# Second attention in pairs of key chunks, with 46 of its 302 score rows in two row tiles of TensorE

## The reference

```python
h = _layernorm(x, gamma, beta)
Q = (h @ Wq).reshape(B, NQ, N_HEADS, HEAD_DIM)          # 16 heads of 64
K = (context @ Wk).reshape(B, NC, N_HEADS, HEAD_DIM)
V = (context @ Wv).reshape(B, NC, N_HEADS, HEAD_DIM)
attn = jnp.einsum('bihd,bjhd->bhij', Q, K)
attn = jax.nn.softmax(attn, axis=-1) * scale             # scale after the softmax
vals = jnp.einsum('bhij,bjhd->bihd', attn, V).reshape(B, NQ, INNER)
return x + vals @ Wo + bo
```

## Time and profile before

| | |
|---|---|
| runs, median (lowest to highest) | 1092.0 us (1091.74 to 1093.75) |
| profiled execution, its own time | 1092.7 us |
| its span, first to last instruction | 1090.9 us |
| mean granted TensorE clock | 0.963 |
| busy: TensorE, its weight loads | 1011.2 us (93%), 738.5 us (68%) |
| busy: VectorE, ScalarE, GpSimd | 742.7 us (68%), 566.7 us (52%), 377.8 us (35%) |
| score passes of the second attention (lines 1281 to 1283) | 384 each |

### The profile page before, as it was taken

One profiled execution on the slowest core, in us unless ns is written; L12 is line 12 of the kernel. 1 busy time (PEld: TensorE's weight loads), 2 busy tenths in 40 slices (PEclk: granted clock), 3 DMA queues, 4 the chain that ended last, 5 costly groups with the idle time before them and its releaser, 6 DMA issues. The chain is left out here.

```text
span 1090.9 us, 31627 instructions
## 1 busy us (share of the span) xinstructions
PE 1011.2 (93%) x12044; PEld 738.5 (68%) x12044; DVE 742.7 (68%) x1406; ACT 566.7 (52%) x1135; POOL 377.8 (35%) x273
## 2 busy tenths in 40 slices
PE   5956999999999999889679999999999999999997
PEld 2642677777777777646327777777777777777786
DVE  4846888778887787311796676767677676767752
ACT  2632777677776776631444444444445444445442
POOL 4612111121111213020106554445555454555542
PEclk8976999999999999979799999999999999999998
DMA  3504444543445432120021211111011111111100
GB/s 117 129 13 132 130 136 143 146 135 121 133 141 149 136 101 87 31 71 0 1 60 41 57 57 58 43 50 41 35 57 55 55 39 53 39 37 57 35 4 4
DMA packets 47022, 79.90 MB, mean 73 GB/s; under 512 B 6979, under 2 KB 33813, under 8 KB 46965
## 3 DMA queue, kind: packets, MB, share of 16 engines
q1 hardware_dynamic: 46964, 79.11, 24.5%
HBM read 50.93 MB, written 21.96 MB: 67 GB/s over the span
## 5 line engine op out<-in xcount | busy, mean ns | idle before, releaser
L1374 ACT ACTIVATE P<-PS 125x448 f32<-125x448 f32 x384 | 207.1, 544 | 265.1 <-PE PS L1283 263.2
L1264 POOL TENSOR_TENSOR Pl<-P 125x896 f16<-125x896 f32 x128 | 229.9, 1801 | 237.0 <-ACT P L1374 237.0
L1010 DVE TENSOR_REDUCE m<-PS 128x1 f32<-128x500 f32 x336 | 220.6, 674 | 114.9 <-PE PS L1001 113.0
L916 DVE TENSOR_REDUCE m_part<-PS 128x1 f32<-128x500 f32 x336 | 210.3, 672 | 60.5 <-PE PS L818 58.9
L1299 PE MATMUL PS<-cNh,P 125*128 125x97 f16 x1344 | 198.0, 208 | 0.1
L1301 PE MATMUL PS<-cNh,Pl 125*128 125x97 f16 x1344 | 197.4, 207 | 0.0
L1300 PE MATMUL PS<-cNl,P 125*128 125x96 f16 x1344 | 196.8, 206 | 0.0
L894 ACT ACTIVATE Pb<-PS 125x448 f32<-125x448 f32 x384 | 186.0, 547 | 19.7 <-PE PS L793 18.7
L1300 PEld LDWEIGHTS PS<-cNl,P 125*128 125x128 bf16 x1344 | 131.9, 98 | 25.4
L818 PE MATMUL PS<-KH,Qmx 128*128 128x500 f16 x336 | 129.4, 387 | 14.2 <-PEq L690 8.2
L1299 PEld LDWEIGHTS PS<-cNh,P 125*128 125x128 bf16 x1344 | 131.1, 98 | 15.7 <-issue 3.2
(11 more groups left out here) (167 smaller groups left out, 1489.0 us busy)
## 6 DMA issues: line engine op xcount, KB each, us to landing
Kst<-k_halves SPq DMA_DIRECT2D x144, 125.0 KB, 2.8
k_halves<-KH SPq DMA_DIRECT2D x16, 750.0 KB, 3.3
cx<-in_ctx SPq DMA_DIRECT2D x16, 562.5 KB
d_cx<-in_ctx SPq DMA_DIRECT2D x16, 562.5 KB
c_halves<-cHi SPq DMA_DIRECT2D x16, 281.2 KB, 2.7
c_halves<-cLo SPq DMA_DIRECT2D x16, 281.2 KB, 3.1
cTh<-c_halves SPq DMA_DIRECT2D x16, 281.2 KB, 3.1
cTl<-c_halves SPq DMA_DIRECT2D x16, 281.2 KB, 4.0
```

The costliest lines, as they stand in the source:

```text
L916: nc.vector.tensor_reduce(m_part[:, t, part:part + 1], PS[:, 6 + k % 2, 0:SP], AX.X, ALU.max).then_inc(s_reduced, 1)
L1010: nc.vector.tensor_reduce(m21[:, t, part:part + 1], PS[:, S1[k % 2], 0:SP], AX.X, ALU.max).then_inc(n_red, 1)
L1264: nc.gpsimd.tensor_tensor(Pl[:, c % NP], P1[:, c % NP], high, ALU.subtract).then_inc(n_low_p, 1)
L1374: nc.scalar.activation(P1[:, c % NP, half * HALF:(half + 1) * HALF], PS[0:KC, u % 3, 0:HALF], ACT.Exp).then_inc(n_exp, 1)
```

## The change

- Scores: the 96 high-by-high, 96 high-by-remainder and 96 remainder-by-high rows and the 14 rows of the maximum are packed anew. Two passes have 128 rows (kA by qA, kB by qB). The last 32 rows of the remainder keys with the high queries, and the 14 rows of the maximum, are a third pass of 46 rows. It stands in partitions 0 to 45 for the first half of the columns and in 64 to 109 for the second; kC holds the keys twice. Tiles of 64 rows by 128 columns are chosen by these partitions.
- Loads: with this packing a batch has 12 loads instead of 4; the two that the maximum pieces read are issued first, ten smaller ones follow.
- Order: chunks go in pairs (six groups). A group is eight full passes, then the 46-row passes of both chunks, then the values of the pair before. Score halves use four PSUM banks, 0 to 3. The maximum pieces use banks 7 and 6, at places written in a table. After the sixth group only the turned maximum and the values of the last pair are left.
- Batch's ends: the next batch's first three score halves no longer wait for the laid maximum. Both transposes of the batch before come in group 0 with a bank each (6 and 7), both copies follow on ScalarE after that group's exponentials, the remainders and the projection come in group 1.
- Maximum: the top of each query is written to PSUM and both f16 parts are made from there, by three VectorE instructions; the constant LIFT moves into the exponential's bias. The turn is one f16 matmul with 128 output rows.
- Pl: VectorE takes chunk 3 alone, GpSimd the other eleven. The memory for the larger buffers comes from weight buffers of the middle stage that share space.

```diff
+        kA = sb_in(late, "kA", [128, 2, SK], F16)
+        kB = sb_in(late, "kB", [128, 2, SK], F16)
+        kC = sb_in(late, "kC", [96 + MR, 2, SK], F16)
-        O1, W1, S1 = 4, 6, (3, 7)
+        O1, W1 = 4, (6, 7)
+        S0, S1 = (3, 7), (7, 6)
...
+            if half == 0:
+                keys(kA, 0, 0, 0, DC)
+            else:
+                keys(kA, 96, 0, 0, 32)
+                keys(kB, 0, 0, 32, 64)
+                keys(kB, 64, 1, 0, 64)
+                keys(kC, 0, 1, 64, 32)
+                keys(kC, 64, 1, 64, 32)
...
+        PLACES = [(0, 0, 0, 0, 0, 0), (0, 0, 0, 0, 2, 0), (1, 0, 1, 1, 1, 1), (1, 0, 1, 1, 1, 1), (1, 0, 1, 1, 1, 1), (1, 1, 1, 1, 0, 0), (0,) * 6]
-        low_on_dve = [c % 3 == 2 for c in range(NC)]
+        low_on_dve = [c == 3 for c in range(NC)]
...
+                def score(i, par, u):
+                    if u == 0:
+                        pe.wait_ge(n_in[1][par], i * LOADS[1] + LOADS[1])
+                    if u == 2 * GC - 1:
+                        pe.wait_ge(n_mlaid, n + 1)
-                    wait_for(pe, n_exp, n * 2 * NC + u - 2)
+                    wait_for(pe, n_exp, n * 2 * NC + u - 3)
-                    o = PS[0:KC, u % 3, 0:HALF]
-                    pe.matmul(o, cTh[:, par, at], Qh[:, par, cols], start=True, stop=False)
-                    pe.matmul(o, cTh[0:DC, par, at], Ql[:, par, cols], start=False, stop=False)
-                    pe.matmul(o, cTl[:, par, at], Qh[0:DC, par, cols], start=False, stop=True).then_inc(n_st, 1)
+                    o = PS[0:KC, u % 4, 0:HALF]
+                    pe.matmul(o, kA[:, par, at], qA[:, par, cols], start=True, stop=False)
+                    pe.matmul(o, kB[:, par, at], qB[:, par, cols], start=False, stop=True)
+                def score_rests(par, g):
+                    for c in range(GC * g, GC * g + GC):
+                        at = slice(c * KC, (c + 1) * KC)
+                        for half in range(2):
+                            rows_of, cols = slice(64 * half, 64 * half + 32 + MR), slice(64 * half, 64 * half + HALF)
+                            mm = pe.matmul(PS[0:KC, (2 * c + half) % 4, 0:HALF], kC[rows_of, par, at], qC[rows_of, par, cols],
+                                           start=False, stop=True, skip_group_check=True)
+                        mm.then_inc(n_st, 2)
...
+                    def pieces(g, place):
+                        these = BESIDE1[g][place]
+                        if par == 0 and g == 1 and place >= 4:
+                            these = (place - 4,)
+                        for k in these if has_b and has_1 else ():
+                            if has_old and k == 0:
+                                pe.wait_ge(n_ot, b * 2)
+                            if has_old and k == 1 and par == 0:
+                                pe.wait_ge(n_y, i)
+                            score_piece1(pe, i, par, k, S1)
+                    for g in range(NG + 1):
+                        if has_1 and g == NG:
+                            turn_maximum(i, par)
+                        if has_b and g < NG:
+                            for j in range(2 * GC):
+                                score(i, par, 2 * GC * g + j)
+                                if j < 3:
+                                    pieces(g, j)
+                            score_rests(par, g)
+                        if has_b and has_old and g == 0:
+                            turn_output(b - 1, 0)
+                            turn_output(b - 1, 1)
+                        pieces(g, 3)
+                        for j in range(GC):
+                            if has_b and g > 0:
+                                values(i, par, GC * (g - 1) + j, tuple(range(QT)))
+                            if has_b and has_old and par == 0 and g == 1 and j == 0:
+                                project(i - 1)
+                            pieces(g, 4 + j)
...
+                        for u in range(2 * GC * g, 2 * GC * (g + 1)) if has_b else ():
+                            act.wait_ge(n_st, b * 2 * NC + 2 * c + 2)
+                            nc.scalar.activation(P1[:, c % NP, half * HALF:(half + 1) * HALF], PS[0:KC, u % 4, 0:HALF], ACT.Exp, bias=lift[0:KC, 0:1]).then_inc(n_exp, 1)
...
+                        if has_b and has_old and g == 0:
+                            keep_old(i, par, 0)
+                            keep_old(i, par, 1)
...
+                        top1 = PS[:, W1[1], 0:QT]
+                        nc.vector.tensor_reduce(top1, m21[:], AX.X, ALU.max).then_inc(n_mlink, 1)
+                        nc.vector.tensor_scalar(mn1[:, :, 32:32 + QT], spread(top1, 1, 2), -1.0, None, ALU.mult).then_inc(n_mlink, 1)
+                        nc.vector.scalar_tensor_tensor(out=mn1[:, :, 32 + QT:32 + MR], in0=spread(top1, 1, 2), scalar=-1.0, in1=mn1[:, :, 32:32 + QT],
+                                                       op0=ALU.mult, op1=ALU.subtract).then_inc(n_mready, 1)
```

More of the change, by code:

```diff
@@ L22 @@
+import itertools
 from contextlib import ExitStack
@@ L976, in program, with keys, queries @@
         n_st, n_fill, n_red, n_mlink = sem("n_st"), sem("n_fill"), sem("n_red"), sem("n_mlink")
-        O1, W1, S1 = 4, 6, (3, 7)
+        O1, W1 = 4, (6, 7)
+        S0, S1 = (3, 7), (7, 6)
         PIECES1 = [(t, part) for part in range(NSP) for t in range(QT)]
+        LOADS = (32, 160)
         def load_halves(sp, i, par, half, queries_made=None, ahead=False):
             slot, n = (par + 1) % 2, i * 2 + par + 1
[L986 to L990, removed]
+            at, loaded = bass.ds(n, 1), n_in[half][slot]
+            def keys(to, first, part, source, count):
+                sp.dma_start(to[first:first + count, slot:slot + 1, :],
+                             c_halves[at, part, source:source + count].rearrange("b p k -> p b k")).then_inc(loaded, 16)
+            def queries(to, first, part, source, count, at_col=0, heads=slice(0, H)):
+                cols = slice(at_col, at_col + (heads.stop - heads.start) * SQ)
+                sp.dma_start(to[first:first + count, slot, cols].rearrange("p (h q) -> p h q", q=SQ).unsqueeze(1),
+                             QK[source:source + count, part, at, heads]).then_inc(loaded, 16)
+            if half == 0:
+                if not ahead:
+                    wait_for(sp, n_st, (n - 1) * 2 * NC)
+                keys(kA, 0, 0, 0, DC)
[5 more added lines that the diff above has]
+                keys(kC, 64, 1, 64, 32)
@@ L996, in score_piece1 @@
+        def score_piece1(pe, i, par, k, banks):
             slot, n = (par + 1) % 2, i * 2 + par + 1
@@ L1221, in turned_parts @@
             cut, rest = divmod(4 * 128, SQ)
-            src = PS[0:DC, W1]
+            src = PS[0:DC, W1[k]]
             if k == 0:
@@ L1264, in body @@
                             nc.gpsimd.tensor_tensor(Pl[:, c % NP], P1[:, c % NP], high, ALU.subtract).then_inc(n_low_p, 1)
-                        if inside(i, par, 1) and c == 4:
+                        if inside(i, par, 1) and c == 3:
                             slot, n = (par + 1) % 2, b + 1
@@ L1326, in turn_maximum @@
                     pe.wait_ge(n_mready, n + 1)
[L1327 to L1331, removed]
+                    pe.matmul(PS[:, W1[0], 0:128], mn1[:].rearrange("p a c -> p (a c)"), ident16[:], start=True, stop=True).then_inc(n_mturned, 1)
                 def body(i, par):
@@ new lines, in lay_maximum @@
+                        for first, t in ((32, 0), (96, QT - 4)):
+                            m = nc.vector.tensor_tensor(qC[first:first + MR, slot].rearrange("p (t q) -> p t q", t=4),
+                                                        spread(PS[first:first + MR, W1[0], 0:128], 1, 4),
+                                                        spread(tab[first:first + MR, C_MM + t:C_MM + t + 4], 2, 128), ALU.mult)
+                        m.then_inc(n_mlaid, 1)
+                    for g in range(NG + 1):
+                        pieces = list(itertools.chain(*BESIDE1[g])) if has_b and has_1 else []
+                        if has_b and has_old and g == 1:
+                            split_old(i, par, 0)
+                            split_old(i, par, 1)
+                        if has_b and has_old and par == 0 and g == 1:
@@ L1471, in body @@
+                        for k in pieces[2:]:
+                            reduce_piece1(dve, i, par, k, S1)
+                        if has_1 and g == NG:
                             lay_maximum()
```

161 lines of the change are left out of this document (66 added, 95 removed).

## The result

The changed kernel takes 1109.78 us, median of four runs (1108.73 to 1111.32), beside 1092.88 us for the one before, measured beside it: ratio 1.015, 95% interval 1.0135 to 1.0165. It is slower, by 17 us, and lies above the stated range (1079 to 1104). Its profiled execution took 1109.35 us with a span of 1107.6, 16.7 us longer than before.

What follows compares the result with a forecast made beforehand. The prediction took TensorE's queue of passes in the second attention as the bound. Seven pairs +1.2, last batch +0.9, start -1.2 and end -1.7 us gave -0.8, so 1091 us (range 1079 to 1104).

Steps and rivals of the forecast that it cites:

- the walk: Second attention's chain summed through tail, head and middle: odd batches 30.65 us, even 33.33, a pair 0.17 longer than before.
- Saved pass, tile changes: TensorE scores: 5 passes a chunk instead of 6 saves 2.28 us a batch; 12 tile changes cost about 0.095 each.
- Rival 1: Tile changes on TensorE cost little, 0.03 instead of 0.1 us: 10 us less, 1081; chance 0.27.
- The bias operand ... keep counts and sizes: Second attention's exponential with its new bias operand, and the middle stage's moved weights: costed at nothing.
- R1: Start of the 46-row passes in a batch's second group; forecast 3.04 us after those of the first group.
- R0: Start of the 46-row passes in a batch's first group, 1.63 us after the batch's start; the number counts groups.
- The port conflict ... nothing waits for: The conflict avoided by splitting the maximum from PSUM stretches a VectorE step nothing waits for today: costed at nothing.
- The tail: Batch's end, from the last group's 46-row passes: 5.88 us, with TensorE waiting twice for GpSimd, 0.7 us each.
- Once-only terms: Outside the repeating batches: start -1.2 us, last batch +0.9, end -1.7.
- Rival 4: Waits and tile changes cost 0.15 rather than 0.10 us: 9 us more, 1100; chance 0.19.
- Rival 2: TensorE's clock falls after idling at batch ends: 1104 to 1117 us, about 1111; chance 0.09.
- Rival 3: The 46-row passes run one after the other, not side by side: 30 us more, 1121; chance 0.05.

Runs made afterwards that it cites:

- e4: Changed kernel with both 46-row passes of a chunk in the lower row tile, one behind the other: 1135.11 us, ratio 1.0383 to the kernel before.
- e1: Changed kernel with the second attention's exponential called without its bias operand, LIFT left out: 1094.88 us, ratio 1.0021 to the kernel before.
- e2: Changed kernel with GpSimd's subtraction for the next context after chunk 5 instead of chunk 3: 1097.85 us, ratio 1.0043 to the kernel before.
- e3: Changed kernel with the low part of chunk 11 on VectorE, behind the maximum: 1098.2 us, ratio 1.0049 to the kernel before.
- e5: Changed kernel with the next batch's first two score halves moved into the tail's first hole: 1098.14 us, ratio 1.0055 to the kernel before.

## Why the prediction was wrong

Direction, size and range were wrong: "the same, 1091" against 15 per mille more. The mechanism was the right one, namely that the saved pass is paid back by TensorE standing at the batch's ends; three terms of the walk were too small.

- **Saved pass, tile changes.** 2.28 us a batch for the pair side by side holds (e4). I took 0.09 in and 0.10 out, which holds (0.10 and 0.09); what I had not is 0.05 more between the two pairs of a group. In the groups that TensorE bounds this makes some 0.15 us a batch, 2 us in all. Rival 1 (0.03) is out. The Trainium skill (TensorEngine Tiling (Array Packing), Key Properties) says that a switch of mode drains the engine; the trace agrees in so far as there and back costs 0.24 us for f16 row tiles. That the change of tiles alone, without other edits, costs this was read from traces, not tried.
- **"The bias operand ... keep counts and sizes": the step that failed first.** I costed it at nothing and walked with a 0.54 us exponential, 0.50 apart. It is 0.636, 0.525 apart. Against my walk R1 comes at R0+3.32 (835.77 to 839.09) instead of 3.04 and the tail is 6.06 instead of 5.88: some 0.9 us a pair, 6 us in all. Without the operand the tail is 5.88, as walked. Against what ScalarE does without it, it is more: e1 gives 12 us in the batches, of which 5 are port waits that it shortens.
- **"The port conflict ... nothing waits for": the step that failed most.** I looked at the conflict that goes (the maximum's parts, 1.69 us at worst before) and not at those that come. GpSimd's context remainder now runs while VectorE makes chunk 3's low part (odd) and Z (even), each with two inputs from SBUF. Measured against the walk: R2 to R3 is 5.44 instead of 4.99 in odd batches (812.36 to 817.80), of which e2 gives back 0.40, and R0 to R2 of an even batch is 11.92 (835.77 to 847.69) instead of 10.64, of which e2 gives back 1.10. Some 1.5 us of the pair's 2.57, 10 us in all. Before, Z took 0.29 us in all eight cases:

```profile
791.24 0.29 DVE L1425 TENSOR_TENSOR Z<-Y,X 112x128 f32<-112x128 f32 x1 [0.24 <-DVE Y L1421]
```

- **The tail.** Its two waits were foretold as 0.7 and 0.7 and are 0.70 and 0.56; e3 and e5 show that each is worth what it says.
- **Once-only terms.** Start -1.6 (forecast -1.2), last batch +1.2 (+0.9), end -1.7 (-1.7). The start can't be told from chance: in e1 to e3, whose edits lie inside the stage, the first reciprocal comes at 602.05, 604.29 and 605.26, and the half clock of 574.0 to 577.4 before is absent from this execution of the changed kernel (574.00 to 577.50 at 1.00).
- **Rivals.** Rival 4 had the sign and the kind (each wait a little dearer) but 9 us instead of 18, and from hand-overs and changes, not from the operand and the port. Rival 2 did not occur: the granted clock stays at 1.00 from batch to batch although TensorE idles 1.3 us in each tail. It falls to 0.50 only in the last projection, as before the change. Rival 3 is refuted by the trace and by e4.

The range was too narrow on the slow side, since it held errors of the terms that I had and none for terms costed at nothing; two of those were the cause.

## What to carry to other kernels

When passes are taken off the engine that bounds a kernel by an order with less running ahead, every duration of the engines behind it moves onto the critical path: price the chain of hand-overs between them with the new operands, and take intervals from stretches where the engine was not waiting. For each operation that changes its place, list what runs beside it on the engine that shares its port. Fill the hole at a batch's end with the next batch's independent work; here that and three small moves turned +1.5% into -1.9%.

## What was not expected of the hardware

- A per-partition bias operand on the 125x448 exponential: 0.636 against 0.548 us, start to start 0.525 against 0.434, also in the kernel before (0.633).
- VectorE's 112x128 addition of two SBUF tensors: 0.29 us alone, up to 1.57 beside GpSimd's 2.29 us subtraction.
- A change from full rows to two 64-row tiles in f16, 448 columns: 0.10 us in, 0.05 between the first pair and the second, 0.09 out.
- The last projection, the same 48 matmuls: 5.20 us at a granted clock of 0.50, 2.73 at 1.00 (e1). Why an execution gets the one or the other stays open, so 2.5 us between two kernels can't be put down to an edit unless the batches show it.
